# Two attention prologues reordered: first rows spread from the columns, first q moved forward, GpSimd's bias additions moved

## The chip, the cores and the metric

One core of a Trainium2 chip runs the whole program. The metric is device time in microseconds (us) of one execution; lower is better.

## The reference, cut to what matters

The program is a chain of five blocks on x of 1024 nodes by 512 values: a graph diffusion, a mixture of experts, two graph attention layers, and a second mixture of experts. Only the two attention layers are touched. With HEADS = 8 each of them computes

```python
h = (x @ W).reshape(N, heads, out_ch)
a_src = jnp.einsum('nhc,hc->nh', h, att_src)
a_dst = jnp.einsum('nhc,hc->nh', h, att_dst)
e = jax.nn.leaky_relu(a_src[src] + a_dst[dst], NEG_SLOPE)
m = jax.ops.segment_max(e, dst, num_segments=N)
ex = jnp.exp(e - m[dst])
s = jax.ops.segment_sum(ex, dst, num_segments=N)
out = jax.ops.segment_sum(h[src] * (ex / s[dst])[:, :, None], dst, num_segments=N)
return out.reshape(N, heads * out_ch) + bias
```

The first layer has 128 values a head (its output goes through relu), the second 64. The second layer's log_softmax is added to x, and x then goes on into the last block; the kernel adds the second layer's bias to x ahead of time.

## The kernel before, in words

The graph is held as dense 1024 by 1024 counts in eight tiles of 128 source nodes, so a head is eight steps; head and step together are a pair, 64 pairs in a layer. `attend` (L2097) writes the program of one layer for each engine. It is called twice: "a1" (L2605, first layer, `final` false) and "a2" (L2608, second layer, `final` true). Each engine runs its own list in the order written, and they meet only at semaphores (`wait_ge`).

When a layer starts, `ab` lies ready in SBUF: for each node (128 partitions by 8 tiles) its 8 source scores and 8 target scores, as columns. What the prologue has to make of it:

- On TensorE, eight transposes (L2460) turn `ab` into rows in PSUM banks 4 and 5. ScalarE copies these to `aTs` (L2336), and TensorE waits for that copy (L2462).
- `a_row(hd)` (L2464) puts the source scores of one head on all 128 partitions, 1024 values each, in two PSUM banks. For heads 0 and 1 it is one matmul per half row from `aTs`, 16 rows deep (L2476). For later heads it uses `a3`, a bfloat16 split of `aTs` into three parts (L2471); ScalarE and GpSimd make it in turns (L2339, L2257, L2342, L2263, L2345, L2347).
- VectorE takes the largest score of each node's neighbours, `maxed(hd, t)` (L2392): eight passes for head 0, eight for head 1, then pair by pair those of the later heads.
- GpSimd makes of head 0's maxima the column `q` (L2236, five small operations). `q_row(0)` on TensorE (L2547, matmuls on L2552) spreads it over the partitions, with eight matmuls whose stationary operand is one column repeated 128 times and whose moving operand is the identity. ScalarE copies it to `qb` (L2353).
- TensorE makes the first H0 units of h = x @ W (`h_tile`, L2480, matmuls on L2483): 3 units in a1, 6 in a2; ScalarE moves each from PSUM (`h_moved`, L2326, copy on L2331). The other units of h are made between the pairs, at the places in `H_AT`.
- SyncE writes `aTs` to memory and reads target scores back, spread over the partitions, as `adb`; from head 1 on it does the same with `q`.

TensorE's order in a layer is: transposes, wait for `aTs`, `a_row(0)`, then unit 0, `a_row(1)`, and the other units, with `q_row(0)` after unit 1 in a1 and after unit 2 in a2 (L2565). Then it waits for all H0 units to be moved and for all 16 maxima (L2567 to L2569) and enters the pairs, where the first thing is `a_row(2)`.

A pair goes: GpSimd adds `am` = CT + `qb` (L2278; a ring of four buffers), ScalarE makes the relu of `adb` plus a column (L2300), VectorE adds both and marks it (`counted`, L2402, L2405), ScalarE takes exp (L2307), and TensorE multiplies it with h (`gather`, L2498, in a1; `columns`, L2511, in a2). VectorE's list between two `counted` holds the maxima of a later head; the one after `counted(0)` is `maxed(2, 0)`, which needs `a_row(2)`.

In a2 GpSimd also adds the layer's bias to the eight tiles of x (`bias_in`, L1627, on L1630): tiles 0 to 4 between the two subtractions that make `a3`, tiles 5 to 7 after q of head 0. VectorE waits for all eight at the start of head 6 (L1877).

Before each layer all engines meet at a barrier (`phase()`, L2604, L2607).

Of the kernel before, what the change touches and what calls it, by code (L numbers as in the profile page):

```python
# [16 lines left out]
P = 128  # L17
# [6 lines left out]
def build(nc, ins, out):  # L24
# [4 lines left out]
    NT = N // P  # L29
# [6 lines left out]
    HEADS, CH1 = ins["L1_gnn_att_src1"].shape  # L36
# [10 lines left out]
    with ctx:  # L47
# [2049 lines left out]
        def attend(tag, KI, CH, xT, W, h, bias_d, adr, qdr, final):  # L2097
# [19 lines left out]
            def row_bank(hd):  # L2117
                return SECOND if hd == 1 else 6

            def unit_bank(i):  # L2120
                return i % 2 if final else (0, 3, 0)[i]
# [8 lines left out]
            if final:  # L2130
                UNITS = [[(t, 0, slice(0, FH), slice(0, FH))] for t in range(NT)] + quarters
                H0 = 6
                H_AT = (0, 1), (0, 3), (1, 1), (1, 5), (2, 1), (2, 5), (3, 5), (4, 1), (4, 5), (5, 1)
            else:
                UNITS = [[(NT - 1, 0, slice(0, FH), slice(0, FH))], [(NT - 1, 1, slice(0, FQ), slice(0, FQ))],
                         *([(t, 2, slice(0, FQ), out) for t, _, _, out in unit] for unit in quarters[NT // 2:])]
                H0 = 3
# [57 lines left out]
            with nc.Block() as block:  # L2195
# [34 lines left out]
                @block.gpsimd  # L2230
                def _(pool):
                    def link(ins, n, s=s_qc):
                        ins.then_inc(s, 1)
                        pool.wait_ge(s, n)

                    def q(hd):  # L2236

                        pool.wait_ge(s_max, NT * hd + NT)
                        a_dst = ab[:, :, HEADS + hd:HEADS + hd + 1].rearrange("p t o -> p (t o)")
                        link(pool.tensor_tensor(zx[:], mrow[:, hd % 2, :], a_dst, ALU.add), 4 * hd + 1)  # L2240
                        link(pool.tensor_scalar(zy[:], zx[:], 0.0, SLOPE - 1, ALU.max, ALU.mult), 4 * hd + 2)
                        link(pool.tensor_tensor(zx[:], zx[:], zy[:], ALU.add), 4 * hd + 3)
                        link(pool.tensor_tensor(zx[:], a_dst, zx[:], ALU.subtract), 4 * hd + 4)
                        wait(pool, s_qrow, 16 * (hd - 2))
                        pool.tensor_scalar(q4[:, hd % 2, :], zx[:], 1 / (SLOPE - 1), None, ALU.mult).then_inc(s_q, 1)

                    pool.memset(h[:, :, :, CH:CH + 1], 1.0).then_inc(s_ones, 1)
                    if final:
                        tail.ones(pool)
                    pool.memset(a3[:], 0.0)  # L2250
                    pool.memset(sel[:], 0.0).then_inc(s_sel, 1)
                    pool.wait_ge(s_sel, 1)
                    for at in (0, 32, 64):
                        own = slice(at, at + 2 * HEADS)
                        pool.tensor_copy(sel[own, :], ident[own, own]).then_inc(s_sel, 1)
                    pool.wait_ge(s_high, 1)
                    pool.tensor_tensor(rest[:], aTs[:], a3[0:2 * HEADS, :], ALU.subtract).then_inc(s_rest, 1)  # L2257
                    if final:
                        pool.wait_ge(s_sel, 4)
                        pool.wait_ge(s_rest, 1)  # L2260
                        tail.bias_in(pool, 0, 5)
                    pool.wait_ge(s_mid, 1)
                    pool.tensor_tensor(rest[:], rest[:], mid[:], ALU.subtract).then_inc(s_last, 1)  # L2263
                    pool.wait_ge(s_bm, 1)
                    q(0)
                    if final:
                        pool.wait_ge(s_last, 1)
                        pool.wait_ge(s_q, 1)
                        tail.bias_in(pool, 5, NT)
                    pool.wait_ge(s_a3, 1)  # L2270
                    for k in range(PAIRS):
                        hd, s = k // NT, k % NT
                        if k == 0:
                            pool.wait_ge(s_q0m, 1)
                        elif s == 0:
                            pool.wait_ge(s_qb[hd % 2], 16 * (hd // 2 + hd % 2))
                        wait(pool, s_exp, k - RING + 1)
                        pool.tensor_tensor(am[:, k % RING, :], CT[:, s, :], qb[:, hd % 2, :], ALU.add  # L2278
                                           ).then_inc(s_sum, 1)
                        if k in Q_AFTER:  # L2280
                            q(Q_AFTER[k])
                        if not final and s == 5 and hd >= 2:
                            pool.wait_ge(s_a2m, hd - 1)
                            if hd == 2:
                                pool.tensor_copy(ab2[:], a2p[:, 0, :]).then_inc(s_a2s, 1)
                            else:
                                pool.wait_ge(s_a2s, hd - 2)
                                pool.tensor_tensor(ab2[:], ab2[:], a2p[:, hd % 2, :], ALU.add).then_inc(s_a2s, 1)
                    if final:
                        tail.pool_end(pool)  # L2290

                @block.scalar
                def _(act):
# [32 lines left out]
                    def h_moved(i, bank):  # L2326
                        act.wait_ge(s_h, i + 1)
                        t, half, columns_in, _ = UNITS[i][0]
                        tiles, heads = len(UNITS[i]), (columns_in.stop - columns_in.start) // CH
                        first = half * HEADS // 2 + columns_in.start // CH if half < 2 else HEADS - 2  # L2330
                        act.copy(h[:, t:t + tiles, first:first + heads, 0:CH],  # L2331
                                 PS[:, bank, 0:tiles * heads * CH].rearrange("p (t h c) -> p t h c", h=heads, c=CH)
                                 ).then_inc(s_hm, 1)
# [13 lines left out]
                    act.copy(a3[64:64 + 2 * HEADS, :], rest[:]).then_inc(s_a3, 1)  # L2347

                    act.activation(warm[:], ident[:, 0:1], ACT.Exp)
                    for i in range(2, H0 - 3):  # L2350
                        h_moved(i, unit_bank(i))
                    act.wait_ge(s_q0, 1)
                    act.copy(qb[:, 0, :], RELU).then_inc(s_q0m, 1)  # L2353
                    if not final:
# [1 line left out]
                    act.wait_ge(s_bm, 2)  # L2356
                    act.wait_ge(s_q0m, 1)
                    relu(0)
                    for i in range(max(2, H0 - 3), H0 - 1 if final else H0):
                        h_moved(i, unit_bank(i))  # L2360
                    for k in range(PAIRS):
                        hd, s = k // NT, k % NT
                        if k + 1 < PAIRS:
                            relu(k + 1)
                        exp(k)
                        if final and k == 0:
                            h_moved(H0 - 1, unit_bank(H0 - 1))
                        if (hd, s) in H_MOVED:
                            h_moved(H_MOVED[hd, s], 3)
                        if final and s == 0 and hd:  # L2370
                            moved(hd - 1)
                        if not final and s == 6 and hd:
                            out(hd - 1, 0)
                        if not final and s == 1 and hd >= 2:
                            out(hd - 2, 1)
                        if not final and s == 3 and hd >= 2:
                            next_moved(hd - 2)
# [78 lines left out]

                @block.tensor
                def _(pe):
                    for t in range(NT):
                        mm = pe.transpose(PS[0:2 * HEADS, 4 + t // 4, (t % 4) * P:(t % 4 + 1) * P], ab[:, t, :], ident[:])  # L2460
                    mm.then_inc(s_a, 1)
                    pe.wait_ge(s_am, 1)  # L2462

                    def a_row(hd):  # L2464


                        wait(pe, s_max, NT * (hd if hd > 2 else hd - 1))
                        if hd >= 2:
                            pe.wait_ge(s_a3, 1)
                            for half in range(2):  # L2470
                                mm = pe.matmul(PS[:, row_bank(hd) + half, :], sel[0:A3, hd:hd + 1].to_broadcast([A3, P]),  # L2471
                                               a3[0:A3, half * 512:(half + 1) * 512], start=True, stop=True)
                            mm.then_inc(s_as, 1)
                            return
                        for half in range(2):
                            mm = pe.matmul(PS[:, row_bank(hd) + half, :], ident[0:2 * HEADS, hd:hd + 1].to_broadcast([2 * HEADS, P]),  # L2476
                                           aTs[:, half * 512:(half + 1) * 512], start=True, stop=True)
                        mm.then_inc(s_as, 1)

                    def h_tile(i, bank):  # L2480
# [73 lines left out]
                        mm.then_inc(s_q0, 1)  # L2554

                    a_row(0)
                    if final:
                        pe.wait_ge(s_w2[0], 16)
                    for i in range(H0):
                        wait(pe, s_hm, i - 1)  # L2560
                        h_tile(i, unit_bank(i))
                        if i == 0:
                            pe.wait_ge(s_bm, 1)
                            a_row(1)
                        if i == (H0 - 4 if final else 1):  # L2565
                            q_row(0)
                    pe.wait_ge(s_hm, H0)  # L2567
                    pe.wait_ge(s_ones, 1)
# [63 lines left out]
```

## Time and profile before

| | us |
|---|---|
| median of 3 runs | 1190.15 |
| lowest, highest | 1181.32, 1196.16 |
| the profiled execution | 1188.69 |
| its span, first to last instruction | 1187.0 |

Busy in the span: PE (TensorE matmul) 993.9 us, DVE (VectorE) 740.7, POOL (GpSimd) 567.6, ACT (ScalarE) 511.9; PEld is TensorE's weight load, which runs beside its matmuls. a1 begins at about 632 us of the span, a2 at about 844 us. An fp32 matmul shows as two matmul records in the trace. In the rows a number in brackets is the idle time of that engine before it and what ended it; "issue" means that the profile shows no releaser.

### The profile page before, as it was taken

The numbers are of one execution on the slowest core, as the hardware profiler recorded it, in microseconds if no ns is written. First come the engines' busy times: TensorE is split into PE (matmuls) and PEld (weight loads), VectorE is DVE, ScalarE is ACT, GpSimd is POOL, SyncE is SP. The second block draws the span as 40 slices with busy tenths as digits, with TensorE's granted clock in tenths as the row PEclk, the third lists the DMA queues.
The fourth block names the chain that finished last, engine by engine and source line by source line (L and its number), as shares of the span: only waits on it lengthen the run. The fifth ranks groups of instructions, "written<-read, shape, count | busy, mean of one in ns | idle before, by whom it ended". The sixth has DMA issues, their size and how long they took to land. (4 is left out here: it accounts for less than half of the span.)

```text
span 1187.0 us, 16494 instructions
## 1 busy us (share of the span) xinstructions
PE 993.9 (84%) x5310; PEld 652.3 (55%) x5310; DVE 740.7 (62%) x1680; ACT 511.9 (43%) x694; POOL 567.6 (48%) x446
## 2 busy tenths in 40 slices
PE   3999899979589988883798789889888888778897
PEld 1445577778445444441454788778664444334665
DVE  6898669536222222221985899985377787797764
ACT  3233554242111111110233688889257676755322
POOL 1000376500556333313202889998378677774242
PEclk9999899955589999996798899999799999988999
DMA  3000001224669999974201012210102111371550
GB/s 120 1 0 1 1 0 47 96 68 167 214 230 406 406 407 406 396 302 142 87 1 38 19 54 50 77 54 19 48 18 72 36 36 41 97 229 49 164 187 35
DMA packets 72152, 143.01 MB, mean 120 GB/s; under 512 B 25120, under 2 KB 38152, under 8 KB 71952
## 3 DMA queue, kind: packets, MB, share of 16 engines
q1 hardware_dynamic: 61360, 121.07, 28.9%
q0 software_dynamic: 10720, 21.01, 5.1%
q8 instruction: 42, 0.69, 0.3%
q14 instruction: 30, 0.25, 0.1%
HBM read 136.08 MB, written 20.11 MB: 132 GB/s over the span
## 5 line engine op out<-in xcount | busy, mean ns | idle before, releaser
L2278 POOL TENSOR_TENSOR am<-CT,qb 128x1024 f32<-128x1024 f32 x128 | 302.2, 2385 | 32.7 <-ACT PT L2307 15.7
L2300 ACT ACTIVATE PS<-adb,ab 128x1024 f32<-128x1024 f32 x128 | 143.2, 1118 | 92.6 <-DVE am L2405 91.4
L2405 DVE TENSOR_TENSOR am<-PS,am 128x1024 f32<-128x1024 f32 x128 | 156.5, 1222 | 36.0 <-ACT PS L2300 28.9
L2399 DVE CUSTOM_DVE_ANT_0 masked<-PS,mask 128x1024 f32<-128x1024 f32 x128 | 156.2, 1220 | 34.5 <-issue 32.8
L2511 PE MATMUL PS<-PT,h 128*65 128x512 f32 x256 | 132.2, 654 | 34.5 <-ACT PT L2307 23.3
L2307 ACT ACTIVATE PT<-am,as 128x1024 f32<-128x1024 f32 x128 | 145.4, 1136 | 0.3 <-DVE am L2405 0.3
L2498 PE MATMUL PS<-h,PT 128*128 128x129 f32 x1024 | 126.7, 281 | 22.2 <-ACT PT L2307 12.3
L2498 PEld LDWEIGHTS PS<-h,PT 128*128 128x128 f32 x1024 | 119.9, 194 | 30.2 <-issue 18.4
L1167 DVE COPY yo<-PS 128x512 f32<-128x512 f32 x36 | 24.9, 692 | 146.6 <-PE PS L1132 146.6
L2511 PEld LDWEIGHTS PS<-PT,h 128*65 128x65 f32 x256 | 34.4, 148 | 106.8 <-issue 91.5
L1058 POOL DMA_INDIRECT ys_scratch<-yo,r_rowsi x36 | 36.7, 1018 | 117.6 <-PE PS L1102 84.0
L1115 PE MATMUL PS<-w1r,xgT 128*64 128x256 f32 x576 | 71.5, 391 | 18.7 <-DMA w1r<-in_L_ffn_W 18.1
L490 DVE TENSOR_SCALAR oh_src<-iota,eT 128x1024 f16 x150 | 72.6, 484 | 13.9 <-PE PS L702 10.2
L1132 PE MATMUL PS<-w2r,hT 128*64 128x512 f32 x288 | 68.9, 600 | 0.5 <-issue 0.5
L1152 ACT ACTIVATE hb<-PS 128x256 f32<-128x256 f32 x36 | 13.9, 385 | 123.4 <-PE PS L1115 106.9
L702 PE MATMUL PS<-oh_src,oh_dst 128*128 x300 | 66.4, 379 | 0.4 <-issue 0.4
L1115 PEld LDWEIGHTS PS<-w1r,xgT 128*64 128x64 f32 x576 | 38.6, 138 | 50.6 <-DMA w1r<-in_L_ffn_W 27.6
L2483 PEld LDWEIGHTS PS<-W2t,x2T 128*128 128x128 f32 x384 | 55.9, 197 | 11.7 <-issue 7.9
L2483 PE MATMUL PS<-W2t,x2T 128*128 128x128 f32 (+1 forms) x384 | 61.2, 318 | 0.0
L721 PE MATMUL PS<-hi,adj 128*128 128x512 f32 x128 | 51.2, 400 | 4.1 <-DVE lo L545 4.1
L393 POOL TENSOR_SCALAR_AFFINE_SELECT mask<-mask 128x128 bf16<-128x128 bf16 x8 | 3.5, 442 | 102.9 <-ACT mask L586 102.9
L722 PE MATMUL PS<-lo,adj 128*128 128x512 f32 x128 | 50.8, 397 | 0.0
(442 smaller groups left out, 1757.6 us busy)
## 6 DMA issues: line engine op xcount, KB each, us to landing
w1r<-in_L_ffn_W SPq DMA_DIRECT2D x28, 1024.0 KB
w2r<-in_L_ffn_W SPq DMA_DIRECT2D x28, 1024.0 KB
w2r<-in_L_ffn_W SPq DMA_DIRECT2D x16, 512.0 KB
w1r<-in_L_ffn_W SPq DMA_DIRECT2D x16, 512.0 KB
adb<-a_scratch SPq DMA_DIRECT2D x16, 512.0 KB, 3.8
qb<-q_scratch SPq DMA_DIRECT2D x14, 512.0 KB, 4.4
wc<-in_L_gnn_W SPq DMA_DIRECT2D x4, 1024.0 KB, 9.4
w1x<-in_L_ffn_W SPq DMA_DIRECT2D x2, 2048.0 KB, 10.8
```

Source lines behind the costliest of these rows:

```text
L490: dve.tensor_scalar(oh_src[:, bass.ds(slot, 1), c, :], iota[:], eT[:, 0, c, bass.ds(q, 1)], None, ALU.is_equal)
L702: mm = pe.matmul(PS[:, 2 * (t % 2) + h, :], oh_dst[:, bass.ds(slot, 1), c, :], oh_src[:, bass.ds(slot, 1), c, h * 512:(h + 1) * 512], star ...
L1115: mm = pe.matmul(PS[own, 2 + i % 2, 0:H], xgT[:, i % 2, k, own], w1r[:, i % PAIRS0 * 2 + h, k, :], start=False, stop=(k == KD - 1))
L1132: mm = pe.matmul(PS[own, 4 + i % 2, :], hT[:, i % 2, c, own], w2r[:, i % PAIRS0 * 2 + h, c, :], start=(c == 0), stop=(c == HC - 1))
L2278: pool.tensor_tensor(am[:, k % RING, :], CT[:, s, :], qb[:, hd % 2, :], ALU.add).then_inc(s_sum, 1)
L2300: act.activation(RELU, adb[:, hd % 2, :], ACT.Relu, bias=ab[:, s, hd:hd + 1]).then_inc(s_relu, 1)
L2307: act.activation(PT[:, k % PR, :], am[:, k % RING, :], ACT.Exp, bias=as02[:, s, hd:hd + 1], scale=1 - NEG_SLOPE).then_inc(s_exp, 1)
L2399: dve.tensor_tensor_reduce(masked[:], wide(row_bank(hd)), mask[:, t, :], 1.0, -3.0e38, ALU.subtract, ALU.max, mrow[:, hd % 2, t:t + 1]).th ...
L2405: dve.tensor_tensor(am[:, k % RING, :], RELU, am[:, k % RING, :], ALU.add).then_inc(s_all, 1)
L2483: mm = pe.matmul(PS[:, bank, columns_out], xT[:, k, tile * P:(tile + 1) * P], W[half][:, k, columns_in], start=(k == 0), stop=(k == KI - 1))
L2498: mm = pe.matmul(PS[:, d // PER, (d % PER) * (CH + 1):(d % PER + 1) * (CH + 1)], PT[:, (NT * hd + s) % PR, d * P:(d + 1) * P], h[:, s, hd, :],
L2511: mm = pe.matmul(PS[0:CH + 1, half, :], h[:, s, hd, :], PT[:, (NT * hd + s) % PR, half * 512:(half + 1) * 512], start=(s == 0), stop=(s == ...
```

## The change

Three edits in `attend`:

- `a_row` for heads 0 and 1 is built as `q_row` is: eight matmuls, each with one tile's column of `ab` repeated 128 times as the stationary operand and the identity as the moving one. It no longer reads `aTs`. On TensorE `a_row(0)` comes first, and the eight transposes follow it; the wait for `aTs` moves to just before `q_row(0)`.
- In a2 `q_row(0)` comes after unit 1 in place of unit 2, and ScalarE copies `qb` and makes the first relu before it moves units 2 and 3; units 4 and 5 it moves after the first exp.
- In a2 GpSimd adds the bias to tiles 0 to 2 after q of head 0, and to tiles 3 to 7 one by one after the fifth step of heads 1 to 5. No bias addition stands between the two subtractions of `a3` any more.

```diff
@@ GpSimd
                     pool.tensor_tensor(rest[:], aTs[:], a3[0:2 * HEADS, :], ALU.subtract).then_inc(s_rest, 1)
-                    if final:
-                        pool.wait_ge(s_sel, 4)
-                        pool.wait_ge(s_rest, 1)
-                        tail.bias_in(pool, 0, 5)
                     pool.wait_ge(s_mid, 1)
...
                         pool.wait_ge(s_q, 1)
-                        tail.bias_in(pool, 5, NT)
+                        tail.bias_in(pool, 0, 3)
...
                             q(Q_AFTER[k])
+                        if final and s == 4 and 1 <= hd < NT - 2:
+                            tail.bias_in(pool, hd + 2, hd + 3)
@@ ScalarE
                     act.activation(warm[:], ident[:, 0:1], ACT.Exp)
-                    for i in range(2, H0 - 3):
-                        h_moved(i, unit_bank(i))
                     act.wait_ge(s_q0, 1)
...
                     relu(0)
-                    for i in range(max(2, H0 - 3), H0 - 1 if final else H0):
+                    for i in range(2, H0 - 2 if final else H0):
                         h_moved(i, unit_bank(i))
...
                         if final and k == 0:
-                            h_moved(H0 - 1, unit_bank(H0 - 1))
+                            for i in range(H0 - 2, H0):
+                                h_moved(i, unit_bank(i))
@@ TensorE
-                    for t in range(NT):
-                        mm = pe.transpose(PS[0:2 * HEADS, 4 + t // 4, (t % 4) * P:(t % 4 + 1) * P], ab[:, t, :], ident[:])
-                    mm.then_inc(s_a, 1)
-                    pe.wait_ge(s_am, 1)
...
-                        for half in range(2):
-                            mm = pe.matmul(PS[:, row_bank(hd) + half, :], ident[0:2 * HEADS, hd:hd + 1].to_broadcast([2 * HEADS, P]),
-                                           aTs[:, half * 512:(half + 1) * 512], start=True, stop=True)
+                        for t in range(NT):
+                            mm = pe.matmul(PS[:, row_bank(hd) + t // 4, (t % 4) * P:(t % 4 + 1) * P],
+                                           ab[:, t, hd:hd + 1].to_broadcast([P, P]), ident[:], start=True, stop=True)
                         mm.then_inc(s_as, 1)
...
                     a_row(0)
+                    for t in range(NT):
+                        mm = pe.transpose(PS[0:2 * HEADS, 4 + t // 4, (t % 4) * P:(t % 4 + 1) * P], ab[:, t, :], ident[:])
+                    mm.then_inc(s_a, 1)
                     if final:
                         pe.wait_ge(s_w2[0], 16)
                     for i in range(H0):
...
-                        if i == (H0 - 4 if final else 1):
+                        if i == 1:
+                            pe.wait_ge(s_am, 1)
                             q_row(0)
```

## Rows read from the trace of the kernel before

**Rows 1.** Chain that ended last, in order of time, a2's prologue: start us, us, what

```profile
844.66 1.88 PE PS L2460 x8
846.57 1.01 ACT aTs L2336
847.62 3.78 PE PS L2476 x4
...
875.80 4.19 issue
```

**Rows 2.** Timeline, a1's prologue: start us, us, engine, line, operation

```profile
632.23 1.03 PE L2460 MATMUL PS<-ident,ab 128*16 128x128 f32 x8 [0.63 <-PEq L1281]
...
634.36 3.28 PE L2476 MATMUL PS<-aTs,ident 16*128 16x512 f32 x4 [1.09 <-ACT aTs L2336]
...
637.68 1.22 DVE L2399 CUSTOM_DVE_ANT_0 masked<-PS,mask 128x1024 f32<-128x1024 f32 x1 [4.37 <-issue]
...
644.95 2.12 POOL L2263 TENSOR_TENSOR a_rest<-a_rest,a_mid 16x1024 f32<-16x1024 f32 x1 [7.37 <-ACT a_mid L2342]
...
649.49 2.05 PE L2552 MATMUL PS<-ident,q 128*128 128x128 f32 x16 [2.34 <-POOL q L2245]
...
652.74 4.66 POOL L2278 TENSOR_TENSOR am<-CT,qb 128x1024 f32<-128x1024 f32 x2 [3.31 <-ACT qb L2353]
...
658.03 1.22 DVE L2405 TENSOR_TENSOR am<-PS,am 128x1024 f32<-128x1024 f32 x1
...
658.33 0.59 PE L2471 MATMUL PS<-a,sel 80*128 80x512 bf16 x2 [3.34 <-issue]
```

**Rows 3.** Timeline, a2's prologue

```profile
851.45 1.22 DVE L2399 CUSTOM_DVE_ANT_0 masked<-PS,mask 128x1024 f32<-128x1024 f32 x1 [6.46 <-issue]
...
868.35 10.53 PE L2483 MATMUL PS<-W2t,x2T 128*128 128x256 f32 x48
...
872.10 1.23 DVE L2405 TENSOR_TENSOR am<-PS,am 128x1024 f32<-128x1024 f32 x1 [0.22 <-POOL am L2278]
...
879.34 0.61 PE L2471 MATMUL PS<-a,sel 80*128 80x512 bf16 x2 [0.46 <-ACT h L2331]
...
879.78 1.88 PE L2511 MATMUL PS<-PT,h 128*65 128x512 f32 x4
...
879.99 1.22 DVE L2399 CUSTOM_DVE_ANT_0 masked<-PS,mask 128x1024 f32<-128x1024 f32 x1 [6.67 <-issue]
...
884.72 3.27 PE L2511 MATMUL PS<-PT,h 128*65 128x512 f32 x4 [3.06 <-ACT PT L2307]
```

**Rows 4.** Windows: stretch, us, busy of PE, PEld, DVE, ACT, POOL, PEclk, DMA, GB/s

```profile
252.61:256.02 3.41, 3.41 (x17) 2.56 (x16) 0.82 (x2) 2.05 (x5) 0.00 (x0) 0.50 0.00 0
256.02:259.43 3.41, 1.17 (x8) 0.73 (x8) 0.00 (x0) 2.92 (x4) 0.00 (x0) 1.00 0.02 5
632.20:634.90 2.70, 1.58 (x10) 0.95 (x11) 0.98 (x1) 1.57 (x2) 1.72 (x6) 1.00 0.20 2
634.90:641.72 6.82, 6.82 (x9) 2.49 (x8) 3.91 (x11) 0.48 (x1) 2.12 (x1) 0.50 0.49 163
844.66:856.76 12.10, 11.00 (x25) 6.43 (x26) 5.37 (x15) 2.04 (x2) 9.74 (x13) 0.50 0.37 116
856.76:878.90 22.14, 22.12 (x105) 18.07 (x103) 15.78 (x36) 9.31 (x13) 16.20 (x19) 1.00 0.02 1
```

**Rows 5.** Groups by line in the stretch 252.61 to 256.02

```profile
L183 PE MATMUL PS<-ident,xln 128*128 128x128 f32 x17 | 4.1, 420 | 0.0
```

**Rows 6.** GpSimd's bias additions, whole span: duration ns min/median/max, first and last start

```profile
L1630 POOL TENSOR_TENSOR x_res<-x_res,a_bias x8: 1262/1267/1271, 851.0 to 865.8; 128x512 f32<-128x512 f32 x8
```

**Rows 7.** Timeline, a2, end of head 3

```profile
964.17 7.32 POOL L2278 TENSOR_TENSOR am<-CT,qb 128x1024 f32<-128x1024 f32 x3 [0.78 <-ACT PT L2307]
...
970.56 1.23 DVE L2405 TENSOR_TENSOR am<-PS,am 128x1024 f32<-128x1024 f32 x1 [0.17 <-ACT PS L2300]
...
976.58 0.21 POOL L2240 TENSOR_TENSOR zx<-mrow,ab 128x8 f32<-128x8 f32 x1 [2.49 <-DVE mrow L2399]
```

## The prediction

> **What bounds the kernel now.** I read the page first for the shape of the run, then the chain that ended last where a2 begins, then the timelines of both prologues, then windows cut where TensorE's granted clock changes.
>
> The chain of a2's prologue [rows 1] shows what the first edit is about: eight transposes (1.88 us), the copy of `aTs` (1.01), `a_row(0)` (3.78), and only then unit 0 of h. While ScalarE copies, TensorE stands still: 844.66 + 1.87 = 846.53 to 847.62, so 1.09 us. From there on TensorE works without a break until unit 5 of h is done. At 875.80 the chain says only "issue" [rows 1]. The timeline says what it was: VectorE's `maxed(2, 0)` starts at 879.99 after 6.67 us of idling, and just before it TensorE ran `a_row(2)`, at 879.34 for 0.61 us, released by ScalarE's move of a unit of h [rows 3]. `counted(0)` had been done since 872.10 + 1.23 = 873.33. So **a2's prologue ends when TensorE has made six units of h**, not when the first q is ready. The reader is to see that a wait named "issue" has a cause in another engine's row.
>
> a1 is different. VectorE's first maximum starts at 637.68, right after `a_row(0)` (634.36 + 3.28 = 637.64), and `counted(0)` at 658.03 follows 16 maxima without a gap: 20.35 us, or 1.27 each. The first sum of GpSimd began at 652.74 and the pair of them was done at 657.40, so `am` was not late; `a_row(2)` comes at 658.33 and is not late either [rows 2]. **a1's prologue ends with VectorE's 16 maxima**, and these begin when `a_row(0)` ends.
>
> The clock. In a1 the granted clock was 1.00 from 632.20 to 634.90 and 0.50 from there to 641.72; in a2 it was 0.50 from 844.66 to 856.76 and 1.00 afterwards [rows 4]. These are the levels of 2.4 and 1.2 GHz. In both, the clock rose while TensorE ran units of h, and the 16-row matmuls of the old `a_row(0)` ran at the low level all through.
>
> **The change, part by part.**
>
> *The rows of heads 0 and 1.* The new `a_row` is the same work as `q_row`: 16 matmul records of 128 columns, 2.05 us at granted clock 1.00 [rows 2], weight loads included. The old one at full clock would be the same number of columns, so the replacement itself costs about nothing. What goes is what stood before it: transposes and copy.
>
> In a1, `a_row(0)` now starts where the transposes started, at 632.23. At full clock it ends at 632.23 + 2.05 = 634.28, and VectorE begins 0.04 later, as before: 634.32 against 637.68, **3.36 us earlier**. At half clock it takes twice the half-clock time of the eight transposes of a2, 2 x 1.87 = 3.74 (the chain gives 1.88, the timeline 1.87) [rows 1], ends at 635.97, and the gain is 1.67. I take 3.36, because the clock stood at 1.00 when the transposes ran there [rows 4], and keep 1.67 for the range.
>
> Does something else become late in a1? The transposes now end at 634.28 + 1.03 = 635.31, against 632.23 + 1.03 = 633.26, so `aTs` comes 2.05 us later, at about 636.3. Behind it on ScalarE and GpSimd hangs the split `a3`, and q of head 0 is queued behind the second subtraction on GpSimd, which waited 7.37 us for ScalarE's middle part in the profile, started at 644.95 and took 2.12 [rows 2]. That part in turn waits for unit 0 of h, which now starts about 2 us earlier than at 637.64, so the subtraction moves forward, not back. q then waits for eight maxima, 634.32 + 8 x 1.27 = 644.5, as it did before; `q_row(0)`, the copy and the first sum move forward with VectorE by the same 3 us, and 652.74 had about 3 us to spare (655.1 for one sum against 658.03). SyncE's write and read-back of `adb` starts 2 us later too; it is wanted after the copy of `qb`, which released the first sum at 652.74 [rows 2], so some 13 us later even when that is 3.4 earlier. I cost all this at nothing.
>
> *a2.* TensorE starts at 844.66 at half clock. `a_row(0)` takes 3.74, to 848.40, so VectorE begins at 848.44 instead of 851.45, 3.0 us earlier. The transposes end at 850.27, and TensorE no longer waits for the copy. But the end is set by TensorE, so I add up its work at full clock: `a_row(0)` 1.95, transposes 1.03, six units at 10.53 / 3 = 3.51 [rows 3], `a_row(1)` and `q_row(0)` 1.95 each; 27.9 us. To this comes half of the time spent at half clock. For the kernel before the same sum is 27.9 + (12.10 - 1.09) / 2 + 1.09 = 34.5, to 879.2; the row is 878.90 [rows 4], so the sum holds to 0.3.
>
> When does the clock rise? Not later than in the profile (12.1 us after the start) for any reason that I see, and not before the first dense stretch is over. For that the nearest rows are 252.61 to 256.02: at 0.50 TensorE ran only matmuls with a 128 x 128 load and the identity moving, the form of the new `a_row`, and the next stretch has 1.00 [rows 4, 5]. So the new `a_row(0)` may itself bring the clock up, at about 850; or the following unit 0 does, at about 853.4; or it stays at 856.8. The gains are the 1.09 of the wait plus half of the half-clock time saved: with 5.4 us at half clock, 1.09 + (11.0 - 5.4) / 2 = 3.9; with 8.7 us, 1.09 + 1.15 = **2.2**; with 12.1 us, 1.09 - 0.55 = 0.5. I take 2.2 and keep 0.5 and 3.9.
>
> *q ahead of the later tiles (a2).* Moving `q_row(0)` one unit forward only reorders TensorE's list. It makes `qb`, the first sum and `counted(0)` earlier, but `maxed(2, 0)` still waits for `a_row(2)` behind six units, so VectorE will wait there longer than 6.67 us. Worth nothing. Could TensorE now wait for q? Head 0's eight maxima end at 848.44 + 10.2 = 858.6 and q takes 1.5, so 860.1; TensorE is through unit 1 at about 850.3 + 2 x 3.5 + 1.95 + 1.5 (half clock) = 860.7. It just fits; with the early rise it would wait about 1 us, which makes the 3.9 above some 3.0. On ScalarE units 2 and 3 are moved behind the copy and the first relu. Unit 4 needs unit 2's bank, and that is only wanted 3.5 us after unit 2 ends; nothing.
>
> *Bias additions.* Before q, GpSimd loses five of 1.27 us [rows 6]. They were hidden, since the second subtraction waits for ScalarE anyway. The three behind q end at about 860.1 + 3.8 = 863.9, when the copy of `qb` ends at about 863 to 864: at most 0.9, and VectorE's 16 maxima run until 868.8. The five in heads 1 to 5 stand before the sum of the sixth step. In head 3, the tightest, that sum ended at 964.17 + 2.4 = 966.6 and VectorE took it at 970.56: 4.0 us of cover for 1.27. At the end of the head GpSimd idles (2.49 us before q at 976.58) [rows 7] and catches up. Nothing, and 5 x 1.27 = 6.3 if the cover were gone.
>
> **Sum.** -3.4 - 2.2 = -5.6 us. Against the profiled execution's own 1188.69 that is 1183.1. The median of the runs stands 1.46 above that execution, and three runs spread over 15 us; I put the forecast between the two bases, at **1184**.
>
> **The rivals.**
>
> *The clock stays low at both starts.* `a_row(0)` of a1 at half clock (1.67) and no earlier rise in a2 (0.5): -2.2, so 1186.5. For it: in the profile the clock fell at 634.90, only 2.7 us after a1 begins. Against it: it fell there with 16-row matmuls and a wait [rows 2, 4], both of which go.
>
> *TensorE's new wait in a1.* With VectorE ahead, units 0 and 1 of h and `a_row(1)` are done at about 642.7, but q comes at 646.0: a wait of 3.3 us, where it was 2.34. After the wait of 2.34 `q_row` still ran at full clock (2.05 us) [rows 2]; after one of 3.06 in a2, four matmul records of L2511 took 3.27 us where four of the same took 1.88 before it [rows 3]. If the clock falls here, `q_row(0)` takes 3.74 and unit 2 (16 records of 256 columns, 10.53 / 3 at full clock) up to 7.0: 646.0 + 3.74 + 7.0 + 0.6 for its move = 657.3, then `a_row(2)` at 657.9. VectorE wants it at 654.67 + 1.23 = 655.9. a1 then gains about 1.3 in place of 3.4; in all -3.5, so 1185.2. The Trainium skill says the same in "TensorE: Matmul & The Clock Gate", section "HAM oscillation — how this bites in real kernels": waits between bursts of matmuls close the clock gate and the next burst starts cold. By that rule this rival would be the forecast; the row of 3.06 us agrees with it, the row of 2.34 does not.
>
> *Slower: the bias additions end up on the path.* If GpSimd sets the pace in heads 1 to 5, the additions cost 6.3 us, and -5.6 + 6.3 gives 1189.4, slower than before. It decides when a sum of the sixth step comes less than 1.3 us before VectorE wants it; in the profile the least cover is 4.0 us [rows 7].
>
> *The change does not do what it says.* The earlier start is given back later, because waits inside the heads are set by other things: 1188.7. Against it: the first pairs of both layers follow from `counted(0)` and `a_row(2)` alone.
>
> **How the numbers follow.** Forecast (gain 4.4 to 7) 0.50; low clock 0.20; new wait in a1 0.17; bias on the path 0.04; nothing gained 0.09. The forecast's own time is 1182 to 1185; with the rivals and the spread of the runs I give 1177 to 1191. A measurement of this kernel tells about 2% from no change, some 24 us. No case comes near that on either side: faster by over 2% 0.02, within 2% 0.965, slower 0.015.
>
> **What would show it.** Right: in a1 the first L2399 starts about 2 us after the barrier and `counted(0)` some 22.4 us after it (25.8 before); in a2 the first L2399 comes 3.8 us after TensorE's start (6.8 before), VectorE's idle time before `maxed(2, 0)` grows past 6.67, and `a_row(2)` starts about 32.5 us after TensorE's start (34.7 before). Granted clock between 848 and 854 tells which of the three rises it was. Wrong: `counted(0)` of a1 waiting for `am`, `a_row(2)` of a1 later than `counted(0)`, GpSimd named as what VectorE waited for in heads 1 to 5, or a difference of more than 3 us outside the two prologues.

## The result, and the profile after

| | before | after |
|---|---|---|
| median of 16 runs each, same chip | 1188.38 | 1179.40 |
| lowest, highest | 1181.32, 1196.16 | 1176.13, 1182.70 |
| profiled execution | 1188.69 | 1180.25 |
| its span | 1187.0 | 1178.5 |

The ratio is 0.9924, 95% interval 0.9905 to 0.9942: 9.0 us less, 0.8%. The same two kernels on two other chips gave 7.6 and 6.5 us less (experiments 1 and 2 below).

The timeline of a1's prologue after (start us, us, engine, line, operation; it answers to [rows 2]; `a_row(0)` is now L2468, the maxima L2396, `q_row` L2544, `counted` L2402, `a_row(2)` L2463):

```profile
631.83 2.02 PE L2468 MATMUL PS<-ident,ab 128*128 128x128 f32 x16 [0.63 <-PEq L1281]
...
633.90 1.22 DVE L2396 CUSTOM_DVE_ANT_0 masked<-PS,mask 128x1024 f32<-128x1024 f32 x1 [0.99 <-issue]
...
645.75 3.38 PE L2544 MATMUL PS<-ident,q 128*128 128x128 f32 x16 [4.07 <-issue]
...
648.96 3.62 PE L2475 MATMUL PS<-W1t,xT 128*128 128x256 f32 x16
...
654.25 1.22 DVE L2402 TENSOR_TENSOR am<-PS,am 128x1024 f32<-128x1024 f32 x1
...
654.55 0.59 PE L2463 MATMUL PS<-a,sel 80*128 80x512 bf16 x2 [1.97 <-issue]
```

The first maximum comes 2.07 us after TensorE's start, where it came 5.45 after it (637.68 - 632.23). `counted(0)` follows 22.42 us after the start, where it was 25.80. The 16 maxima still run without a gap between. The one new thing is in brackets: TensorE waits 4.07 us for q, and `q_row(0)` then takes 3.38 us in place of 2.05.

The timeline of a2's prologue after (answers to [rows 3]):

```profile
840.76 3.75 PE L2468 MATMUL PS<-ident,ab 128*128 128x128 f32 x16 [2.09 <-PEq L61]
...
844.56 1.22 DVE L2396 CUSTOM_DVE_ANT_0 masked<-PS,mask 128x1024 f32<-128x1024 f32 x1 [3.47 <-issue]
...
846.01 3.89 PE L2475 MATMUL PS<-W2t,x2T 128*128 128x256 f32 x16
...
856.39 2.02 PE L2544 MATMUL PS<-ident,q 128*128 128x128 f32 x16 [1.24 <-issue]
...
864.91 1.22 DVE L2402 TENSOR_TENSOR am<-PS,am 128x1024 f32<-128x1024 f32 x1
...
872.69 0.60 PE L2463 MATMUL PS<-a,sel 80*128 80x512 bf16 x2 [0.47 <-ACT h L2329]
...
873.34 1.22 DVE L2396 CUSTOM_DVE_ANT_0 masked<-PS,mask 128x1024 f32<-128x1024 f32 x1 [7.21 <-issue]
...
878.07 3.65 PE L2503 MATMUL PS<-PT,h 128*65 128x512 f32 x4 [3.06 <-ACT PT L2305]
```

`a_row(2)` comes 31.93 us after TensorE's start (34.68 before), and VectorE idles 7.21 us for it, more than the 6.67 of before: as in [rows 3], this stage ends with TensorE's six units, not with VectorE.

Windows of after, cut where the granted clock changes (stretch, us, busy of PE, PEld, DVE, ACT, POOL, PEclk, DMA, GB/s; they answer to [rows 4]):

```profile
631.80:645.20 13.40, 9.84 (x56) 7.25 (x56) 11.84 (x27) 7.11 (x8) 6.74 (x12) 1.00 0.29 83
645.20:648.60 3.40, 2.85 (x13) 2.89 (x14) 3.27 (x10) 0.51 (x2) 0.36 (x2) 0.50 0.02 5
...
840.76:846.60 5.84, 5.84 (x26) 5.14 (x27) 2.23 (x6) 0.34 (x1) 1.83 (x7) 0.50 0.20 50
846.60:872.60 26.00, 24.38 (x128) 21.26 (x126) 18.83 (x45) 11.55 (x16) 20.90 (x20) 1.00 0.16 44
...
877.30:884.10 6.80, 6.03 (x11) 3.15 (x12) 6.59 (x11) 5.92 (x6) 5.86 (x3) 0.50 0.23 77
```

In a1 the clock is 1.00 (2.4 GHz) through the whole first burst; in a2 it rises from 0.50 (1.2 GHz) to 1.00 5.84 us after the start, where that took 12.1. The last row is in head 0, just behind the prologue: the clock falls again for 6.8 us. In the kernel before it fell at the same place, for 3.4 us:

```profile
884.10:887.50 3.40, 2.78 (x4) 0.94 (x5) 3.30 (x7) 2.81 (x4) 2.73 (x2) 0.50 0.00 0
```

Where the 8.44 us between the spans come from, from the starts of the same instructions in both traces (heads 1 to 5 run from `counted(1, 0)` to `counted(6, 0)`, heads 6 and 7 from there to `counted(7, 7)`):

| stretch | us saved |
|---|---|
| up to a1's start (before the change) | 0.40 |
| a1 (212.43 to 208.93) | 3.50 |
| a2's prologue, to `a_row(2)` (34.68 to 31.93) | 2.75 |
| `a_row(2)` to `counted(1, 0)` (24.04 to 25.67) | -1.63 |
| heads 1 to 5 | 0.55 |
| heads 6 and 7 (56.56 to 53.16) | 3.40 |
| the rest of the program | -0.53 |

### The profile page after: what moved, and what is told of

Its sections match the earlier page's. It is cut to its first block and busy times, and to the rows that moved or that the text cites. A ratio compares the mean times of both kernels' runs of the same rounds, so it can differ in the third digit from the quotient of the medians.

```text
span 1178.5 us, 16589 instructions
## 1 busy us (share of the span) xinstructions
PE 982.3 (83%) x5358; PEld 653.8 (55%) x5358; DVE 738.9 (63%) x1680; ACT 511.6 (43%) x694; POOL 565.3 (48%) x446
## 5 line engine op out<-in xcount | busy, mean ns | idle before, releaser
L2402 DVE TENSOR_TENSOR am<-PS,am 128x1024 f32<-128x1024 f32 x128 | 156.4, 1222 | 36.0 <-ACT PS L2298 29.1
L2396 DVE CUSTOM_DVE_ANT_0 masked<-PS,mask 128x1024 f32<-128x1024 f32 x128 | 156.2, 1220 | 30.3 <-issue 28.6
L2503 PE MATMUL PS<-PT,h 128*65 128x512 f32 x256 | 124.4, 617 | 35.7 <-ACT PT L2305 24.5
L784 POOL DMA_INDIRECT xs_scratch<-xln,r_posi x16 | 15.8, 988 | 72.0 <-DVE r_posi L884 67.4
```

The source lines that it names most:

```text
L2396: dve.tensor_tensor_reduce(masked[:], wide(row_bank(hd)), mask[:, t, :], 1.0, -3.0e38, ALU.subtract, ALU.max, mrow[:, hd % 2, t:t + 1]).th ...
L2402: dve.tensor_tensor(am[:, k % RING, :], RELU, am[:, k % RING, :], ALU.add).then_inc(s_all, 1)
L2503: mm = pe.matmul(PS[0:CH + 1, half, :], h[:, s, hd, :], PT[:, (NT * hd + s) % PR, half * 512:(half + 1) * 512], start=(s == 0), stop=(s == ...
```

## The experiments

My theory: the first edit alone makes the gain, by the two prologues; the q move and the bias additions give nothing. Rivals: the other two edits have a share, or the gain comes from the heads behind the prologues. Times are medians; "first maximum" and "`a_row(2)`" are us after TensorE's start in a1 and in a2. For the kernel before these were 5.45 and 34.68, and heads 6 and 7 took 56.56.

**1 and 2. The changed kernel again, on two other chips** (no edit).

> The changed kernel once more, on the chip of the next three. Theory A (a1 3.7 us, a2's prologue 1.9 to 2.8, and beside these only where half-clock stretches and the collisions of GpSimd's sums with VectorE's additions in heads 6 and 7 fall, which differ from execution to execution): 5.6 to 9 us faster than before, and the last heads of the profile need not look as in the first profile. Theory C (the last heads are lastingly shorter by 2 to 3.4 us): 8 to 9 us faster and (7,4) to (7,5) again 3.5 us, not 6.9.

> The changed kernel a third time, beside the next three on one chip. The prologues alone give a1 3.7 and a2 1.9 to 2.8 us in the profiles so far. Theory A: 5.6 to 8 us faster than before. Theory C (heads 6 and 7 of a2 are lastingly 2 to 4 us shorter): 8 to 10 us, and from the first counted of head 6 to the last of head 7 again 52 to 55 us, against 56.4 to 56.6 with the old rows.

Measured: 1183.66 against 1191.29, ratio 0.9945 (0.9923 to 0.9967), and 1181.45 against 1187.95, ratio 0.9946 (0.9922 to 0.9970). So 7.6 and 6.5 us; the 9.0 was at the upper end. Neither reaches the 8 us that theory C asks for, though heads 6 and 7 were short in both profiles (54.33 and 52.85 us). The profile of experiment 2 shows a case that the prediction kept as a bound. Its timeline at a1's start:

```profile
633.59 3.60 PE L2468 MATMUL PS<-ident,ab 128*128 128x128 f32 x16 [0.63 <-PEq L1281]
...
637.24 1.22 DVE L2396 CUSTOM_DVE_ANT_0 masked<-PS,mask 128x1024 f32<-128x1024 f32 x1 [2.57 <-issue]
```

The same 16 records take 3.60 us here, not 2.02, at granted clock 0.50, and the first maximum comes 3.64 us after the start. Against the profile of before, 1.8 of the 3.4 us are left there, and none at a1's end: a1 took 213.26 us, where before took 212.43. But those are two executions with different clocks. Experiment 5 below has the old rows in a1, and in its profile the clock was low from a1's start too:

```profile
633.89 1.86 PE L2461 MATMUL PS<-ident,ab 128*16 128x128 f32 x8 [0.63 <-PEq L1281]
...
640.67 1.22 DVE L2399 CUSTOM_DVE_ANT_0 masked<-PS,mask 128x1024 f32<-128x1024 f32 x1 [5.70 <-issue]
```

There the first maximum came at 6.78 us and a1 took 216.43. At the same low clock the new rows are thus 3.14 us earlier. Whether the clock is low at a1's start differs between executions of one kernel.

**3. The first edit alone, in both layers.** q's place and the bias additions as before:

```diff
-    transposes; wait for aTs; a_row(0) from aTs
+    a_row(0) from ab's columns; transposes
+    wait for aTs before q_row(0)
```

> Only the first edit, in both layers: rows of heads 0 and 1 from the columns, transposes behind a_row(0); the place of q and the bias additions stay as before. Theory A (the two prologues by their chains, the rest by where the half-clock stretches of the second layer's heads fall): a1's first maximum and its first counted come 3.4 to 3.8 us earlier as in the changed kernel, a2's a_row(2) 2.5 to 2.8 earlier on top of that, and the whole is 5 to 9 us faster than before, ratio about 0.993 to 0.996. Theory B (the part of the gain beyond 6.4 us comes from the q and bias edits): about 6.4 us, ratio 0.9946, and the last heads of a2 as in the kernel before.

Measured: 1181.65 against 1190.37, ratio 0.9935 (0.9911 to 0.9958). First maximum 2.07, as expected; `a_row(2)` 32.53, so 2.15 us earlier than in before, less than the 2.5 to 2.8 expected. The first edit is the whole gain, within what can be measured.

**4 and 5. The first edit in a1 only, and in a2 only.** The same diff, under `if not final` and under `if final`.

> The first edit in the first layer alone. Theory A: VectorE's maxima set a1's end, so counted(0) of a1 comes 3.4 to 3.8 us earlier and the shift is still there at a2's start; a2's prologue is as before (a_row(2) 34.7 us after TensorE's start, up to some 2 us either way by where the clock rises). Whole: 2 to 5.5 us faster, ratio 0.9955 to 0.998. Theory B: 3.7 us within 0.5, as nothing in a2 depends on when it starts.

> The first edit in the second layer alone, the other half of the run with the first layer alone. By the prediction's sum for a2: a_row(2) 1.9 to 2.8 us earlier after TensorE's start than the 33.4 to 34.9 of the kernels with the old rows, a1 as before, and 2 us faster in all (0.5 to 4). Theory C would want heads 6 and 7 at 52 to 55 us here too, and 4 to 6 us in all.

Measured: a1 only 1186.31 against 1190.37, ratio 0.9971 (0.9951 to 0.9992); a2 only 1185.90 against 1187.95, ratio 0.9976 (0.9951 to 1.0000), so for a2 alone the times do not exclude that nothing was gained. By the ratios 3.5 and 2.9 us, 6.3 together, where experiment 3 has 7.7 by its ratio (5.0 to 10.6). In the profiles a1 took 208.31 us with the edit there, and `a_row(2)` of a2 came at 32.53 with the edit there. Both are single executions from the ends of their spreads: that of experiment 4 took 1180.93, 5.4 below its median, and that of experiment 5 took 1192.23, the slowest of its 12. Its a1 was to be as before and took 216.43 us, where before took 212.43.

**6. The bias additions alone.**

```diff
-    bias tiles 0 to 4 between a3's subtractions, 5 to 7 after q
+    bias tiles 0 to 2 after q, 3 to 7 after step 4 of heads 1 to 5
```

> Only the bias additions moved (three behind q of head 0, five in heads 1 to 5). Theory A: GpSimd has 3.4 us and more of cover at every place, so no sum is late for VectorE and the time is that of the kernel before within 1 us. Theory B: 1 to 2 us faster, seen in heads 6 and 7. The rival of the prediction (bias on the path): up to 6.3 us slower.

Measured: 1190.82 against 1190.37, ratio 1.0008 (0.9987 to 1.0030). Nothing that the times show. The timeline of the kernel after, head 3, shows the cover (it answers to [rows 7]):

```profile
958.17 1.27 POOL L1630 TENSOR_TENSOR x_res<-x_res,a_bias 128x512 f32<-128x512 f32 x1
...
959.41 7.00 POOL L2274 TENSOR_TENSOR am<-CT,qb 128x1024 f32<-128x1024 f32 x3
...
965.38 1.22 DVE L2402 TENSOR_TENSOR am<-PS,am 128x1024 f32<-128x1024 f32 x1 [0.22 <-ACT PS L2298]
```

The first of the three sums ends at about 959.41 + 7.00 / 3 = 961.7 and VectorE takes it at 965.38: 3.6 us are left in the tightest head, and what VectorE waited for is ScalarE.

**7. The q move alone**, with ScalarE's new order.

```diff
-    if i == (H0 - 4 if final else 1):
+    if i == 1:
         q_row(0)
```

> Only q_row(0) of a2 one unit earlier, with ScalarE's order. Theory A: counted(0) of a2 is earlier, VectorE idles that much longer before maxed(2, 0), a_row(2) stays within 0.5 us of 34.7 after TensorE's start, the time as before within 1 us. Theory B: 1 to 2 us faster.

Measured: 1191.15 against 1190.37, ratio 1.0011 (0.9996 to 1.0027). `a_row(2)` comes 34.89 us after the start (34.68 before). Nothing alone that the times show. Beside the first edit, this and the bias edit together move `a_row(2)` from 32.53 to 31.93, so 0.6 us at most.

**8. A delay of known size in a1.** VectorE makes two additions of 128 x 1024 (1.23 us each) between `a_row(0)` and the first maximum of a1, in the kernel after. If the prologue's time reaches the end undiminished, this must cost 2.5 us.

```diff
+    if not final:
+        dve.wait_ge(s_as, 1)
+        for j in range(2):
+            link(dve.tensor_tensor(masked[:], CT[:, 0, :], CT[:, 1, :], ALU.add), j + 1, s_delay)
     for hd in range(2):
```

> The changed kernel with two additions of 128 by 1024 on VectorE (some 1.2 us each) ahead of a1's first maximum. VectorE's maxima are the chain of a1: counted(0) of a1 comes 2.4 us later and the time is 2.4 us more than the changed kernel's (2 to 3). If GpSimd's or ScalarE's side set a1's end, as in the prediction's second rival: 0 to 1 us more.

Measured: 1186.67, where the kernel after had 1183.66 on that chip: 3.0 us for 2.5. In the profile the first maximum was at 4.59 and `counted(0)` at 24.94, both 2.52 later, and a1 took 211.35 us, 2.2 more than in experiment 1. So what VectorE gains at a1's start arrives at the end, as far as medians of 12 and 7 runs tell, which spread over 5.9 and 3.8 us.

The same profile shows what TensorE's wait for q can cost in a2, whose code is that of the kernel after. The clock rose 3.12 us after a2's start, TensorE came to `q_row(0)` early, waited 2.31 us, and the clock fell again (a row of the timeline, then a window, columns as above):

```profile
860.09 2.49 PE L2549 MATMUL PS<-ident,q 128*128 128x128 f32 x16 [2.31 <-issue]
...
861.47:864.88 3.41, 3.41 (x12) 2.93 (x12) 3.32 (x8) 2.13 (x2) 3.41 (x3) 0.50 0.00 0
```

`a_row(2)` then came at 33.36 in place of 31.93: 1.43 us later, in spite of the earlier rise.

**9. Work for TensorE where its clock falls in head 0.** 13 matmuls of zeros into an unused bank behind the first `columns` of a2:

```diff
     columns(hd, s) if final else gather(hd, s)
+    if final and k == 0:
+        for _ in range(13):
+            pe.matmul(PS[:, 2, :], onesb[:], zerob[:], start=True, stop=True)
```

> The changed kernel with 13 matmuls of 512 zero columns in an unused bank after the first pair's matmuls of a2, where TensorE waits 3.06 us. Theory A: the wait is filled, the clock does not fall there, and from a_row(2) to the first counted of head 1 it is 22.7 us, as in the kernels whose clock stayed up, in place of 25.7: 0 to 3 us faster than the changed kernel, by how often the clock falls there. If zero operands do not count, or if that stretch does not matter for the end: no difference.

Measured: 1182.74, ratio 0.9943 (0.9919 to 0.9967), as without them (0.9945). The clock did not fall there, and `a_row(2)` to `counted(1, 0)` took 22.68 us in place of 25.67; but experiment 2, without them, took 22.68 too. The unfilled wait stands in eleven profiles, each time 3.06 us long. In four of them the clock fell at its end (before, after, experiments 1 and 7); in seven it stayed up, with old rows and with new ones. The -1.63 of the table thus belongs to some executions and not to the change, and filling the wait bought nothing that the times show.

**10 and 11. `a_row(2)` ahead of units 3 to 5.** The reading of a2's prologue says that VectorE idles 7.21 us for `a_row(2)` because it stands behind six units of h, and `a_row(2)` needs none of them:

```diff
+    if final and i == 2:
+        a_row(2)
...
-    if k in A_ROW:
+    if k in A_ROW and not (final and k == 0):
```

ScalarE moves unit 4 after the first exp and unit 5 after the second.

> The changed kernel with a2's a_row(2) after unit 2 of h in place of behind all six, and ScalarE's move of unit 5 after the second exp. The text says that a2's prologue ends with TensorE's six units and that VectorE idles 7.2 us for a_row(2), so here maxed(2, 0), counted(1) and exp(1) run beside units 3 to 5, TensorE goes from unit 5 into the first pairs without the wait of 3.06 us, and the clock does not fall there: 3 to 6 us faster than the changed kernel, about 1174 to 1177. If VectorE or ScalarE were what ends that stretch: less than 1 us.

> The kernel with a2's a_row(2) after unit 2 once more, beside the changed kernel on the same chip: if its first result holds (profile 6 us shorter up to head 1), it is 3 to 6 us faster than the changed kernel and 9 to 13 us faster than the kernel before. If that was one execution's luck: no more than 1 us from the changed kernel.

Measured: 1180.16 on one chip, where before had 1191.29 and after 1183.66 (ratio to before 0.9916, 0.9887 to 0.9944); 1177.17 on another, where they had 1187.95 and 1181.45 (0.9919, 0.9890 to 0.9948). So 3.5 and 4.3 us below the changed kernel and about 11 below the one before. The 1180.16 misses the 1174 to 1177 that was named for it; the difference to the changed kernel does not miss its 3 to 6. The intervals of the two kernels still overlap on each chip. The timeline of a2's prologue in experiment 10:

```profile
861.82 0.60 PE L2462 MATMUL PS<-a,sel 80*128 80x512 bf16 x2
862.26 10.52 PE L2474 MATMUL PS<-W2t,x2T 128*128 128x256 f32 x48
...
865.03 1.22 DVE L2401 TENSOR_TENSOR am<-PS,am 128x1024 f32<-128x1024 f32 x1
...
866.18 1.22 DVE L2395 CUSTOM_DVE_ANT_0 masked<-PS,mask 128x1024 f32<-128x1024 f32 x1
```

`a_row(2)` runs first and the three units behind it; `maxed(2, 0)` at 866.18 follows `counted(0)` with no idle time in brackets, where 7.21 us stood. `counted(1, 0)` came 51.4 us after a2's start in both profiles, 57.60 in the profile of the kernel after. Of these 6.2 us, 3.0 are the clock's fall in head 0: where a kernel with the old place of `a_row(2)` had none (experiments 2 and 12), `counted(1, 0)` came at 54.6. That leaves 3.2 us for the new order, near the 3.5 to 4.3 of the medians; the wait of 3.06 us, in which the clock can fall, is gone with it.

**12. Half of the feed-forward weights loaded later**, in the kernel after. SyncE loads them in a2 in the same queue as head 7's `qb`; if the landing of `qb` decides heads 6 and 7, this shortens them.

```diff
 def load_early(self, sp, units):
-    sp.wait_ge(self.s_h, units)
-    self.load_w1(sp, 0)
+    self.units = units
 def load_late(self, sp):
+    sp.wait_ge(self.s_h, self.units)
+    self.load_w1(sp, 0)
     self.load_w1(sp, 1)
```

> The changed kernel with the first half of w1x loaded after head 7's qb in place of ahead of it. In the profiles head 7's q write and read-back lie behind that load on the DMA engines and land 19 to 21 us after head 6's first counted. If that landing and its collision with VectorE's additions decide the length of heads 6 and 7, they come out at or under 52.5 us and the kernel is 1 to 3 us faster than the changed one. If TensorE's half-clock stretches decide it alone: 52 to 57 us as in the others, no difference, or slower by the later load (0 to 2 us).

Measured: 1179.56 against 1187.95, ratio 0.9941 (0.9916 to 0.9966); after had 0.9946 there. Head 7's first sum started 17.47 us after `counted(6, 0)`, where the other profiles have 19.2 to 21.05, but heads 6 and 7 took 53.73 us. Up to `counted(7, 4)` they took 43.58 us, the shortest of all profiles (the others 43.98 to 45.78), and the pair behind it 5.15 us, where most have 3.55. So the landing of `qb` does not make the difference between 53 and 56 us; whether it is worth something up to `counted(7, 4)` is not shown.

**All 14 profiles side by side.** The table of the result compares two executions. With the old rows in a1 (before, experiments 5, 6 and 7) the first maximum came at 5.10 to 6.78 us, mean 5.67; with the new ones (nine profiles, experiment 8 with its delay left out) at 2.07 to 3.70, mean 2.43. With the old rows in a2 (before, experiments 4, 6 and 7) the clock rose 9.4 to 12.4 us after TensorE's start and `a_row(2)` came at 33.35 to 34.89, mean 34.08. With the new ones the clock rose after 3.1 to 6.1 us in all ten profiles, and in the six of them with all three edits and the order of the kernel after, `a_row(2)` came at 31.93 five times and once at 33.36 (experiment 8), mean 32.17. By these means the prologues gain 3.24 and 1.91 us, together 5.15.

**What stays open: heads 6 and 7.** They took 56.1 to 56.6 us in all four profiles with the old rows in a1 and 52.5 to 54.3 in all ten with the new ones, though in experiment 4 the code of a2 is that of before. The difference shows at one place, from `counted(7, 4)` to `counted(7, 5)`: 6.84 to 6.91 us in the four; 3.55 in eight of the ten, and 5.21 and 5.15 in experiments 1 and 12. Experiments 5 and 8 are alike to 0.3 us from `counted(6, 0)` up to `counted(7, 4)`; the windows around it (columns as above), of experiment 5:

```profile
1074.20:1077.60 3.40, 1.29 (x3) 0.47 (x4) 3.03 (x14) 3.11 (x4) 1.36 (x1) 1.00 0.00 0
1077.60:1084.40 6.80, 6.80 (x23) 3.77 (x22) 3.32 (x8) 5.42 (x5) 5.71 (x3) 0.50 0.01 2
```

and of experiment 8:

```profile
1069.70:1073.10 3.40, 1.55 (x4) 0.66 (x5) 3.03 (x12) 3.11 (x4) 1.62 (x1) 1.00 0.00 0
1073.10:1076.50 3.40, 3.40 (x23) 2.05 (x22) 2.92 (x6) 2.99 (x3) 3.15 (x3) 1.00 0.02 5
```

The same 23 records take 6.80 us at granted clock 0.50 in the one and 3.40 at 1.00 in the other, after nearly the same work. Why the old rows in a1 went with the first and the new with the second, some 440 us after a1's start, I could not find; with 14 profiles it may also be chance. It also matters which executions were profiled: the profile of experiment 4, short heads, is one of the three fastest of its 12 runs, and that of experiment 5, long heads, is the slowest of its 12. The times leave little room for it: experiment 4 has the shorter heads in its profile and a median only 4.1 us lower (1.0 to 5.8 by its ratio), of which a1's prologue is some 3.

## Why the prediction was right, point by point

- **a1, 3.36 us.** Right: 3.38 at the first maximum and at `counted(0)`, and experiment 8 supports that it reaches the end. The lower bound of 1.67 sets new rows at the low clock against old rows at the high one. The low clock came, in experiments 2 and 9 (first maximum 3.64 and 3.70), but it comes to the old rows too (6.78 in experiment 5), and like against like 3.1 us are left. The reason given against the rival with the low clock does not hold for a1: it was to go with the 16-row matmuls and their wait, but in experiments 2 and 9 the clock fell within 0.2 us of TensorE's start, at the first of the new rows.
- **a2, 2.2 us.** Right in its mechanism: the sum of TensorE's work decided, and the clock rose earlier with the new rows in all ten profiles. In this pair the gain is 2.75; by the means of the profiles it is 1.9. But the case that came is not the one behind the 2.2: the clock rose 5.84 us after the start, near the early case (5.4) and not the one taken (8.7), and TensorE waited for q, 1.24 us against "about 1". That case stood at "some 3.0". That 2.2 lies so close is partly luck.
- **The q move and the bias additions, nothing.** Right (experiments 6 and 7). The rival with a slower end needed a cover under 1.3 us; it was 3.6.
- **TensorE's new wait in a1.** The wait came, 4.07 us for the 3.3 forecast, and the clock fell for `q_row(0)`. In all ten profiles with the new rows in a1 the wait was 4.02 us or more and `q_row(0)` took 3.38 to 3.76 us. The Trainium skill ("TensorE: Matmul & The Clock Gate", section "HAM oscillation — how this bites in real kernels") has it so for waits between bursts of matmuls, in an example with waits of about 3 to 5 us. Here the trace agrees. The row of 2.34 us, which the prediction counts against the rule, is shorter than the waits of that example and is no test of it; the 3.06 us of head 0 went either way. What the prediction had wrong is the rival's price behind the wait, unit 2 at "up to 7.0": the clock was back and unit 2 took 3.62 us. So `a_row(2)` was not late in a1 and the wait cost nothing there. In a2, where TensorE's list ends the stage, `a_row(2)` came 1.4 us later after such a wait in experiment 8.
- **What had no term.** The heads were taken as neutral. In the profile they were not: -1.63 in head 0, +3.40 in heads 6 and 7. The second passes the 3 us outside the prologues that the prediction named as what would make it wrong. Both are changes of granted clock; the first comes and goes between executions, the second is open.
- **Sum.** The prologues measure 3.50 + 2.75 = 6.3 us in this pair, and 5.15 by the means of the profiles, against the 5.6 forecast. The three timed comparisons, 9.0, 7.6 and 6.5, lie above it; 5.6 lies inside the intervals of the last two and below that of the first (6.9 to 11.3 us). The 1179.40 lies inside the range of 1177 to 1191, which was widened for the rivals and the spread of the runs, but below the forecast's own 1182 to 1185, and the 9.0 above its gain of 4.4 to 7. So up to four us of the timed gain are not accounted for. Experiment 3, the first edit alone, has them too; heads 6 and 7 are the one place behind the prologues where the profiles show such a gain, and the times do not bear it out.

## What to carry to other kernels

Before pricing an edit in a start-up stage, find which engine's list ends the stage: here VectorE's maxima in a1 and TensorE's units of h in a2, so the same edit was worth some 3 us in one, and in the other, 2 to 3 us, half of the time that TensorE no longer spent at the low clock and the wait for `aTs`. A long idle time put down to "issue" just behind a row of another engine can be an order to change: moving `a_row(2)` ahead of work that it does not need brought 3.5 to 4.3 us more. A wait that TensorE gains is priced from the clock of the work behind it, one matmul group at a time, and by whose list ends the stage: here it cost nothing in a1, where VectorE's does, and 1.4 us in one profile of a2, where TensorE's does. And profiles are compared at like clocks, or over several executions, before a difference is put down to an edit.

## What was not expected of the hardware

The new `a_row(0)` does not meet the same clock each time: 16 records of the same form and place, behind the same work, took 2.02 us in most profiles of a1 and 3.60 in experiment 2. One wait of 3.06 us, the same in eleven profiles, ended in a fall of the clock in four. After nearly the same work TensorE's clock fell at (7, 4) in one program and not in another, worth 3.4 us there. A single profile of this kernel therefore carries a few microseconds of clock that belong to that execution, as much as half of the effect studied.
